# Masking squared attention scores: GpSimd's select and a triangle matmul replaced by one VectorE instruction

## The reference

```
out = x + attention(xn) + ffn(xn)          # x: 2048 x 1024 on each core

attention: 16 heads, q and k of 16 features, v of 64
  feature map of s = [1, s/2, (s outer s)/(4*sqrt 2)]
  A = tril(features(q) . features(k))      # = 1 + a + a*a/2 with a = q.k/4
  y = A v, then divided by its RMS over the 64, then times Wo
ffn: W1, W2 rounded to {-1, 0, 1} by a threshold (half the mean of |W|), GELU between
```

## Time and profile before

| | |
|---|---|
| time, median of 3 runs | 759.47 us (757.98 to 760.49) |
| profiled execution: time / span of its slowest core (core 5) | 760.95 us / 759.2 us |
| spans of the eight cores | 753.8 to 759.2 us |
| busy share of the span: TensorE, VectorE, ScalarE, GpSimd | 91%, 55%, 32%, 13% |
| attention chunks | from 27 us to 299 us of the span |
| feed-forward part | from 302 us to the end |

### The profile page before, as it was taken

How to read it: one execution, slowest core, us unless ns; L and a number is a source line. 1 busy time by engine, 2 the same in 40 slices (tenths; PEclk the granted TensorE clock), 3 DMA queues, 4 the chain that set the end, 5 groups by cost and what they waited for, 6 DMA issues and landing times.

```text
span 759.2 us, 11498 instructions; the slowest of 8 cores (753.8 to 759.2 us)
## 1 busy us (share of the span) xinstructions
PE 691.8 (91%) x4050; PEld 335.8 (44%) x4050; DVE 417.8 (55%) x623; ACT 243.4 (32%) x322; POOL 99.1 (13%) x131
## 2 busy tenths in 40 slices
PE   2777888877789888999999999999999999999998
PEld 1344544544445444444444444444444444444443
DVE  6667564678577566276556435351554554401653
ACT  3456666657557443222333333333100000000000
POOL 3112222224122211000000001010010000000000
PEclk9999999999999999999999999999999999999999
DMA  7974464766848624659786614533353676200883
GB/s 155 204 161 103 87 122 92 171 146 194 216 143 261 201 69 128 171 198 303 216 281 175 213 56 131 200 114 110 111 200 133 206 223 195 98 1 20 244 232 115
DMA packets 65415, 121.49 MB, mean 160 GB/s; under 512 B 22096, under 2 KB 28112, under 8 KB 65360
## 3 DMA queue, kind: packets, MB, share of 16 engines
q1 hardware_dynamic: 46752, 64.46, 28.0%
q0 software_dynamic: 18608, 56.30, 27.2%
HBM read 103.30 MB, written 16.78 MB: 158 GB/s over the span
## 4 chain that ended last, share of the span: by engine, by line
PE 81%; ACT 6%; DMA 5%; issue 4%; DVE 2%; POOL 2%; SPq 0%; ACTq 0%; DVEq 0%; POOLq 0%
PE pST L1199 8%; PE pY L1221 7%; PE pSS L1199 7%; PE pST L1221 7%; PE pW L1199 7%; PE pW L1221 7%; PE pSS L1221 7%; PE pY L1199 7%; PE pSS L977 4%; PE pW L1134 4%; PE pW L977 4%; PE pSS L1134 3%; ACT Am L922 3%; DMA xr<-x 2%; PE pSS L966 2%
## 5 line engine op out<-in xcount | busy, mean ns | idle before, releaser
L1221 PE MATMUL pY<-w2t,hT 128*128 128x512 bf16 x256 | 66.0, 379 | 0.1
L1221 PE MATMUL pST<-w2t,hT 128*128 128x512 bf16 x256 | 66.0, 379 | 0.0
L1221 PE MATMUL pSS<-w2t,hT 128*128 128x512 bf16 x256 | 66.0, 379 | 0.0
L1221 PE MATMUL pW<-w2t,hT 128*128 128x512 bf16 x256 | 66.0, 379 | 0.0
L524 POOL TENSOR_SCALAR_AFFINE_SELECT Am<-Am 128x1024 bf16<-128x1024 bf16 x32 | 35.3, 1104 | 208.4 <-ACT Am L922 208.4
L1199 PE MATMUL pST<-xnT,w1t 128*128 128x512 bf16 x272 | 61.5, 379 | 0.0
L1199 PE MATMUL pSS<-xnT,w1t 128*128 128x512 bf16 x256 | 57.9, 379 | 0.4 <-DVE consts L705 0.4
L1199 PE MATMUL pW<-xnT,w1t 128*128 128x512 bf16 x256 | 57.9, 379 | 0.0
L1199 PE MATMUL pY<-xnT,w1t 128*128 128x512 bf16 x240 | 54.2, 379 | 0.0
L719 DVE TENSOR_SCALAR w1t<-stg,consts 128x2048 bf16<-128x2048 f32 (+1 forms) x18 | 21.0, 1165 | 54.1 <-PE pY L1199 53.9
L517 POOL DMA_DIRECT2D stg<-w1r x32 | 25.1, 784 | 163.3 <-DVE w1t L722 147.5
(11 more groups left out here) (185 smaller groups left out, 1043.0 us busy)
## 6 DMA issues: line engine op xcount, KB each, us to landing
stg<-w1r POOLq DMA_DIRECT2D x32, 1024.0 KB, 7.5
stg<-w2r SPq DMA_DIRECT2D x16, 1024.0 KB, 9.0
stg<-w2r POOLq DMA_DIRECT2D x16, 1024.0 KB, 7.1
xr<-x SPq DMA_DIRECT2D x16, 512.0 KB, 5.2
res_scr<-rst SPq DMA_DIRECT2D x16, 512.0 KB, 3.2
res<-res_scr SPq DMA_DIRECT2D x32, 256.0 KB, 3.6
xs<-x SPq DMA_DIRECT2D x32, 256.0 KB, 3.9
out<-osb SPq DMA_DIRECT2D x32, 256.0 KB, 2.5
```

The source lines that it names most:

```text
L1221: return e.matmul(out_bank(n), hT[:, j, 128 * t:128 * t + 128], w2t[8 * dh + j // 4][:, j % 4, :], start=(j == 0), stop=(j == NJ - 1))
```

## The change

The mask and the one half become one VectorE instruction, `Am = (Am + 0.5) * tril`, with `tril` a triangle of ones. The select on GpSimd and the matmul of the triangle on TensorE go. GpSimd now waits for VectorE's semaphore `dMK` before it issues the chunk's transfers. VectorE's instruction stands after the layer-norm statistics and ahead of the scaling of chunk i-1. Since the triangle's matmul was the first of its group, the flag that starts the PSUM group moves to the first matmul that is left.

```diff
 # GpSimd, chunk i
-            am = Am[:, i % 2, :, :]
-            unit_emptied(e, ("s", i))
-            e.affine_select(am, am, [[0, 8], [1, 128]], ALU.is_ge, 0.0, base=0,
-                            channel_multiplier=-1).then_inc(gMK, 1)
+            e.wait_ge(dMK, i + 1)
...
 # VectorE, set-up
-        pub(e.tensor_scalar(tril05[:], t2, 0.0, 0.5, ALU.is_ge, ALU.mult))
+        pub(e.tensor_single_scalar(tril[:], t2, 0.0, ALU.is_ge))
...
 # VectorE, chunk i
             if ln_tile(i) is not None:
                 ln_a(ln_tile(i))
+
+            unit_emptied(e, ("s", i))
+            e.scalar_tensor_tensor(Am[:, b, :, :], Am[:, b, :, :], 0.5,
+                                   tril[:].unsqueeze(1).broadcast_to([128, 8, 128]),
+                                   ALU.add, ALU.mult).then_inc(dMK, 1)
             if i >= 1:
                 rms_and_scale(i - 1)
...
 # TensorE, y_before(i)
+            if i % 16 == 0:
+                return
             if i >= 2:
                 e.wait_ge(dNM, i - 1)
-            unit_emptied(e, value_unit(i))
-            e.matmul(yb, tril05[:], values(i), start=True, stop=False,
-                     skip_group_check=True)
-            if i % 16 == 0:
-                return
...
-                         st1[:, g, :], start=False, stop=False,
+                         st1[:, g, :], start=(g == 0), stop=False,
...
 # TensorE, y_within(i)
-            e.wait_ge(gMK, i + 1)
+            e.wait_ge(dMK, i + 1)
+            if i % 16 == 0:
+                unit_emptied(e, value_unit(i))
+                if i >= 2:
+                    e.wait_ge(dNM, i - 1)
             for h in range(8):
                 mm = e.matmul(yb[:, E * h:E * h + E], Am[:, b, h, :],
-                              values(i)[:, E * h:E * h + E], start=False, stop=True,
+                              values(i)[:, E * h:E * h + E],
+                              start=(i % 16 == 0 and h == 0), stop=True,
```

More of the change, by code:

```diff
@@ L242, in build_program @@
     KX = at("KX", [128, 8, 64], BF16, 196.5)
-    tril05 = at("tril05", [128, 128], BF16, 197.75)
+    tril = at("tril", [128, 128], BF16, 197.75)
     tio = at("tio", [128, 8, 16], F32, 198)
@@ L309, in build_program @@
     dL = [S("dL0"), S("dL1")]
-    sIO = S("sIO"); gMK = S("gMK"); sMS = S("sMS"); sSU = S("sSU")
+    sIO = S("sIO"); sMS = S("sMS"); sSU = S("sSU")
     sLB = S("sLB"); sLA = S("sLA"); sLS = S("sLS"); sLR = S("sLR"); sXN = S("sXN")
@@ L319, in build_program @@
     sA1 = S("sA1"); sA1D = S("sA1D"); sA2 = S("sA2"); aG = S("aG")
-    dQM = S("dQM"); dW = S("dW"); dKF = S("dKF"); dRD = S("dRD"); dRC = S("dRC")
+    dQM = S("dQM"); dMK = S("dMK"); dW = S("dW"); dKF = S("dKF"); dRD = S("dRD"); dRC = S("dRC")
     dNM = S("dNM"); dS1 = S("dS1"); sTR = S("sTR"); sTH = S("sTH"); sTC = S("sTC")
```

## The result

The change costs 2.6%: 779.29 us (median of four runs, 778.69 to 781.85) against 759.75 us for the kernel before (757.98 to 760.49), ratio 1.0257, interval 1.0235 to 1.0279. The direction was forecast, the size was not: +19.5 us against +11.5, outside the range of 763 to 777.

A forecast was written before the change was run, and what follows sets the result against it. Attention was taken as bound by square, select, then `y_within`, delays reaching the end one for one. Terms -0.4 + 0.6 + 0.2 + 3.8 + 0.45 + 3.7 + 1.95 + 1.2 = +11.5 us gave 771.0 us, range 763 to 777.

The forecast's parts named there:

- the term for TensorE's clock: New idle stretches in chunks 17, 19, 21, 25 and 31 bring none to three more low-clock stretches: +1.2 us, 0 to 5.
- Chunks 17 to 19: VectorE has next to no pause; late masks and the late load of chunk 18 delay the start of chunk 20: +3.7 us.
- The hold of chunk 17: The mask waits behind VectorE's scaling of Wo until 180.88, so `y_within` starts at 182.24 instead of 178.48: +3.8 us.
- The select of chunk 18 ended at 186.77: The load behind that select went out at 188.70 and would now go out at 192.3, 3.6 us later, delaying ScalarE.
- The other holds: Mask behind long VectorE instructions: chunks 21 and 25 +1.9 us each, chunk 14 +0.45, chunk 31 +1.65, chunk 30 +0.3.
- Chunk 24: One of six chunks with the select on the chain and VectorE free: +0.1 us each.
- What goes: The triangle's matmul, 0.21 us per chunk, mostly covered by the wait for ScalarE's square: -0.4 us in all.
- The mask, 1.23 us: VectorE's mask instruction over 1024 bf16 elements takes 1.23 us, with 0.69 us as the lower end.
- The free chunks: In chunks 15, 16, 20, 22, 24 and 26 the mask is ready 0.1 us later than the select: +0.6 us.
- The rival "VectorE becomes the bound and the clock falls too": VectorE without a pause there adds three masks, plus three more low-clock stretches: +17.3 us, 776.8 us, chance 0.11.

The follow-up runs named there:

- experiment 2: The changed kernel with matmuls of a zero matrix filling TensorE's gaps ahead of `y_within` in chunks 17, 21, 25 and 31: 772.77 us, ratio 1.0163.
- experiment 6: The changed kernel, but GpSimd issues a chunk's transfers after ScalarE's square instead of waiting for the mask: 777.64 us, ratio 1.0226.
- experiment 5: The kernel before, without the triangle's matmul and so without the constant one half: 760.46 against 760.81 us, ratio 1.0002.
- experiment 13: The changed kernel with masks of chunks 17 to 19, 21, 23, 25, 29 to 31 issued early, scalings of Wo in chunks 12, 15, 17: 766.76 us, ratio 1.0076.
- experiments 8 to 11: The changed kernel, masks ahead of long instructions, Wo scalings in chunks 12 to 15; 9, 11 short mask; 10, 11 chunk 16's mask not ahead: 770.41, 761.7, 767.75, 763.85 us.

## Why the prediction was wrong in size

Core 0's later start of the feed-forward part, 20.4 us, taken apart by the shift of each `y_within` from chunk to chunk. Lower clock is the length of a group of 16 matmuls above 3.61 us; shorter groups at the lower clock, as in chunk 18, are left in the other column:

| chunk | held or moved | lower clock |
|---|---|---|
| 14 to 16 | +0.2 | |
| 17 | +4.2 | |
| 18 | +0.8 | +2.3 |
| 19, 20 | +0.9 | |
| 21, 22 | +1.9 | +1.7, +1.7 |
| 23, 24 | +1.5 | |
| 25, 26 | +2.1 | +1.3 |
| 27 to 31 | +2.1 | +1.3, and -1.7 for one of before |
| sum | 13.7 | 6.6 |

The prediction had most of the holds and their places right, and three terms too small. Its terms add up to 11.5 us, the table to 20.3. Of the 8.8 us between them the clock is 5.4, chunks 17 to 20 are 2.1, chunks 23 and 24 are 1.2, and all else is 0.1.

- **The step that failed is above all the term for TensorE's clock, +1.2 (of 0 to 5).** It measured 6.6 us on core 0 by the table and 6.5 us by experiment 2. The forecast named the places (17, 19, 21, 25, 31) and took a fifth of what came. On core 5 it is 3.4 net.
- **Second, every term was read from core 5, and the sum put on its time** ("The profiled execution has a span of 759.2 and a time of 760.95; it would come to 772.4"), since it was the slowest. But in that execution it was the slowest because it had already waited 4.24 us for a load and lost 1.7 us of clock in chunk 20, and after the change that wait is 1.82 us and that group at full clock: the old losses took up part of the new ones. Cores without that slack lost up to 21.8 us, overtook it, and the metric is the slowest core. That core 5's first feed-forward matmul came 11.6 us later does not confirm the sum of 11.5: from chunk 11 on it was 13.8, and the difference is about what the clock had been taken too small by.
- **Chunks 17 to 19, +3.7.** On core 5 `y_within(20)` came 3.8 us later, on the others 6.8 to 10.2; 2.3 of core 0's 8.5 is clock. The hold of chunk 17 itself was well sized (+3.8 forecast, +4.2 on every core). The step "The select of chunk 18 ended at 186.77" was core 5's, 1.4 us later than core 0's (184.30 + 1.09): on core 0 the load behind it moved from 187.90 to 195.93 us, 8.0 and not 3.6, and on core 5 to 194.56, 5.9.
- **The other holds.** Chunk 21 +1.8 and chunk 25 +1.9 (1.9 each forecast), chunk 14 +0.4 (0.45), chunk 31 +1.5 with a gap of 4.21 us (1.65). Right.
- **Chunk 24**, +1.4 on core 0, was put down as free: there ScalarE waits 2.79 us for a load. Experiment 6 prices the late loads at some 2 us in all.
- **What goes.** The matmul: forecast -0.4, and nothing that can be measured by experiment 5.
- **The mask, 1.23 us**: 1.216. The trace agrees with section 5.1 of "Vector Engine (DVE) Microarchitecture Reference" of the Trainium skill, which lists the mode of two elements per cycle for `tensor_tensor` and not for this opcode; the section "What auto-detection actually checks" of its "VectorE: DVE Perf Modes", taken by itself, would have had 0.69.
- **The free chunks**, +0.1 each: the gap ahead of `y_within` is 0.62 instead of 0.51 us. Right.
- The rival "VectorE becomes the bound and the clock falls too" (776.8 us, chance 0.11) came nearest in its time, and by the clock in its mechanism; that VectorE itself bounds chunks 17 to 19 no experiment shows by itself. It deserved more: the earlier trace rows had shown VectorE without a pause.

Open stays why the cores differ in their waits for loads of the same size and in when they reach chunk 11, and what makes up core 0's loss in chunks 17 to 20 of experiment 13. That the copies and `ytm` come later by the length of a mask would fit, but no kernel here takes that apart.

## What to carry to other kernels

When a chip's time is that of its slowest core, work the sum out for a second, undisturbed core as well: the slowest one can have, as here, the very slack that hides your cost. An instruction moved to an in-order engine costs what stands ahead of it as well as its own length; look for the long ones there, and put it ahead of them, but watch what you push back (experiments 8 to 11). And count a gap of 2 to 4 us on TensorE with the slow stretch behind it, on core 0 1.3 to 2.3 us each time; on core 5 three of the four gaps had one.

## What the runs showed of the hardware

- Additional matmuls with zeros made the kernel 6.5 us faster: with 52 of them on idle time the granted clock was 0.987 to 0.991 by core, where it was 0.977 to 0.982.
- `scalar_tensor_tensor` over bf16 alone took 1216 ns for 128x1024, `tensor_tensor` 683.
- Without GpSimd's select beside them, VectorE's two-input roundings of half a block (L718) took 1.28 us in chunks 29 to 31, where they had taken 1.91 to 1.92, and four scalings of Wo 1.67 us, where those that overlapped the select had taken 2.02 (core 0) and 2.52 (core 5). In each of these two groups of four one scaling ran long, and it overlapped the select: 0.83 and 1.31 us against 0.48. The scalings have one large input, so the slowing beside GpSimd was not confined to instructions with two.
